# A graph network's second layer, written out: counts on four column groups, 15 block buffers in place of 6, two blocks used where they lie

## The reference

```python
h = maximum(layernorm(x), 0)
for W, b in ((W0, b0), (W1, b1)):              # the two layers
    h = hyp_linear(h, W, b)
    xt = logmap0(h)
    msg = xt[src] * w[:, None]
    agg = segment_sum(msg, dst)                # the sums over edges
    h = hyp_act(expmap0(agg))
x = x + h
h = maximum(layernorm(x), 0)
e = relu(concat([h[src], h[dst]]) @ W1 + b1) @ W2 + b2
counts = segment_sum(ones_like(dst), dst)      # edges of each destination
x = x + segment_sum(e, dst) / clip(counts, 1)
```

## Time and profile before

| | |
|---|---|
| time, median of 3 runs | 1238.22 us (1237.97 to 1239.96) |
| the profiled execution: its time, its span | 1235.21 us, 1233.2 us |
| TensorE busy | 1074.5 us (87%) |
| VectorE busy | 845.4 us (69%) |
| ScalarE busy | 598.8 us (49%) |
| second layer's groups, from first to last instruction | 529.5 to 651.7 us |
| mean traffic with HBM | 139 GB/s |

### The profile page before, as it was taken

How to read it: one execution, slowest core, us unless ns; L and a number is a source line. 1 busy time by engine, 2 the same in 40 slices (tenths; PEclk the granted TensorE clock), 3 DMA queues, 4 the chain that set the end, 5 groups by cost and what they waited for, 6 DMA issues and landing times.

```text
span 1233.2 us, 53744 instructions
## 1 busy us (share of the span) xinstructions
PE 1074.5 (87%) x22532; PEld 997.0 (81%) x22532; DVE 845.4 (69%) x1141; ACT 598.8 (49%) x1693; POOL 27.5 (2%) x28
## 2 busy tenths in 40 slices
PE   2089898988989888389997779999999999999998
PEld 2068777777777776279996579999999999999997
DVE  8889999999999995655555844444444444444442
ACT  5358888888888886300001643333333333333331
POOL 7000000000000000100000000000000000000000
PEclk9589999999999999689997779999999999999999
DMA  2003323223232233369970344444444444444440
GB/s 78 0 32 123 121 91 121 106 106 121 91 121 113 100 121 125 148 243 365 373 280 28 110 150 158 155 155 155 155 154 155 153 155 146 152 149 147 148 139 28
DMA packets 45160, 171.75 MB, mean 139 GB/s; under 512 B 19472, under 2 KB 19798, under 8 KB 45115
## 3 DMA queue, kind: packets, MB, share of 16 engines
q1 hardware_dynamic: 45115, 171.12, 38.7%
HBM read 122.95 MB, written 48.14 MB: 139 GB/s over the span
## 4 chain that ended last, share of the span: by engine, by line
PE 54%; DVE 30%; issue 8%; ACT 4%; DVEq 3%; DMA 0%; POOL 0%; ACTq 0%; POOLq 0%
PE PS L1419 17%; PE PS L1432 13%; PE PS L1421 11%; PE PS L1301 7%; DVE arena L963 6%; DVE arena L940 5%; DVE arena L948 4%; PE PS L1329 3%; DVE arena L926 3%; DVE arena L935 2%; DVEq L330 2%; ACT arena L594 1%; PE PS L1286 1%; PE PS L1377 1%; DVE Cw L755 1%
## 5 line engine op out<-in xcount | busy, mean ns | idle before, releaser
L1419 PE MATMUL PS<-arena 125*128 125x128 bf16 x3600 | 345.2, 219 | 6.8 <-ACT RT L699 6.3
L707 ACT ACTIVATE arena<-PS 128x512 f32<-128x512 f32 (+1 forms) x336 | 180.1, 551 | 319.5 <-PE PS L1421 319.5
L1164 DVE TENSOR_TENSOR arena<-ramp,slot_dst 128x1800 f32<-128x1800 f32 x48 | 97.6, 2033 | 251.2 <-PE PS L1432 250.7
L1419 PEld LDWEIGHTS PS<-arena 125*128 125x128 bf16 x3600 | 250.7, 97 | 10.8 <-issue 7.2
L1301 PE MATMUL PS<-arena,A 125*64 125x72 f32 x4800 | 177.8, 229 | 67.0 <-DVE aggTw L974 38.9
L1301 PEld LDWEIGHTS PS<-arena,A 125*64 125x64 f32 x4800 | 164.0, 138 | 76.5 <-DVE A L844 27.0
L594 ACT ACTIVATE arena<-arena 128x72 bf16<-128x72 bf16 x864 | 217.0, 344 | 1.9 <-DVE arena L948 1.9
L1421 PE MATMUL PS<-arena 108*128 108x128 bf16 x1200 | 167.4, 220 | 0.0
L1421 PE MATMUL PS<-arena,HTw 108*128 108x128 bf16 x1200 | 166.1, 219 | 0.0
L1432 PE MATMUL PS<-arena 128*64 128x72 f32 x4800 | 160.6, 227 | 0.4 <-DVE RT L1200 0.4
L1432 PEld LDWEIGHTS PS<-arena 128*64 128x64 f32 x4800 | 153.5, 137 | 5.5 <-DVE RT L1200 0.6
(11 more groups left out here) (182 smaller groups left out, 1048.1 us busy)
## 6 DMA issues: line engine op xcount, KB each, us to landing
adjacency<-arena SPq DMA_DIRECT2D x48, 900.0 KB, 3.6
arena<-adjacency SPq DMA_DIRECT2D x48, 900.0 KB, 5.2
Bw<-slot_rows SPq DMA_DIRECT2D x48, 800.0 KB, 4.2
Cw<-slot_rows SPq DMA_DIRECT2D x48, 700.0 KB, 4.9
arena<-q_table SPq DMA_DIRECT2D x144, 18.0 KB
q_table<-arena SPq DMA_DIRECT2D x6, 336.0 KB
slot_rows<-slot_row SPq DMA_DIRECT2D x49, 13.0 KB
x_sb<-in_x SPq DMA_DIRECT2D x1, 700.0 KB
```

The lines of the kernel that those rows point to most:

```text
L707: nc.scalar.activation(Hs[k][:, bs[0]:bs[-1] + 1, :], ts_ps[(k + q) % 2][:, 0:len(bs), :], ACT.Relu)\
L1164: nc.vector.tensor_tensor(Os[k], ramp[:, 1:1 + W].unsqueeze(1).broadcast_to([128, NB, W]), slot_dst[:, bass.ds(g, 1), :].rearrange("p g b ...
L1419: mm(ps, OTs[k][:, b, :], P3[:, b, part, :], start=(part == 0), stop=False)
```

## The change

The second layer is written out for all 48 groups on SP, TensorE and VectorE, and its order and buffers change:

- Groups 46 and 47 come first, and their blocks are read from `AB`, where the first layer left them (`KEPT`). The other 46 are loaded, in order, into 15 buffers in place of 6. These lie in the arena in front of and behind `AB`, over tables that only the first layer uses.
- The one-hots and their offsets (`OC`, `offb`) move from the arena into `Cw`.
- VectorE makes the one-hots of group i + 1 before it adds the sums and counts of group i.
- A count matmul has 32 columns of ones in place of one and writes to one of four 32-partition quarters of PSUM, in turn. There are two PSUM banks for the counts. `degree` becomes all 128 partitions of `RT`; its total is the sum of partitions 0, 32, 64 and 96, which the transposing matmuls of the end form with a vector `first_of`. There are 50 of these in place of 25.

```diff
-SECOND = 6
+SECOND = 15
-        degree = RT[0:1, :]
+        degree = RT[:, :]
+        kept = at[0] - 2 * NB * W
+        starts = list(range(0, kept - NB * W + 1, NB * W)) + list(range(at[0], ARENA - NB * W + 1, NB * W))
+        ABS = [arena[:, i:i + NB * W].rearrange("p (b w) -> p b w", w=W) for i in starts[0:SECOND]]
+        KEPT = [(g, AB[g % 2]) for g in (NG - 2, NG - 1)]
+        OC = [Cw[:, i * GT * HW:(i + 1) * GT * HW].bitcast(bf16).rearrange("p (t w) -> p t w", w=W) for i in range(2)]
-        cnt_ps = bank(3)[0:1, 0:W]
+        cnt_ps = [bank(2 + k)[:, 0:W] for k in range(2)]
...
+        def second_group(i):
+            return KEPT[i][0] if i < len(KEPT) else i - len(KEPT)
+        def second_buffer(i):
+            return divmod(i - len(KEPT), SECOND)
...
+            def load_blocks(i):
+                n, k = second_buffer(i)
+                if n:
+                    sp.wait_ge(applied2, nth(i - SECOND))
+                sp.dma_start(ABS[k].rearrange("p b w -> p (b w)"), a_d[second_group(i), :, :]).then_inc(a_in[k], 16)
...
+            ve.tensor_reduce(first_of[:, :], ident[:, 0:128:32], X, ALU.add)
...
-                def body(g, _, n, k):
-                    ve.wait_ge(cone_set, nth(g - 2))
+                def count_onehots(i):
+                    k = i % 2
+                    if i >= 2:
+                        ve.wait_ge(counted, nth(i - 2))
...
+                def add_group(i):
+                    base = window(ve, second_group(i))
+                    ve.wait_ge(applied2, nth(i))
+                    ve.wait_ge(added2, 2 * i + PRIMED)
...
+                count_onehots(0)
+                for i in range(NG):
+                    if i + 1 < NG:
+                        count_onehots(i + 1)
+                    add_group(i)
...
-                pe.wait_ge(added2, 2 * g + PRIMED)
+                if i >= 2:
+                    pe.wait_ge(added2, 2 * i - 2 + PRIMED)
                 for t in range(GT):
-                    last = mm(cnt_ps, onesb[:, 0:1], OC[k][:, t, :], start=(t == 0), stop=(t == GT - 1))
+                    quarter = slice(32 * (t % 4), 32 * (t % 4) + 32)
+                    last = mm(cnt_ps[k][quarter, :], onesb[:, 0:32], OC[k][:, t, :], start=(t < 4), stop=(t >= GT - 4))
...
             for b in range(NB):
-                last = mm(PS[0:PN, 3584 + b:3585 + b], degree[:, 0:N].rearrange("f (p b) -> f b p", b=NB)[:, b, :],
-                          ones[0:1, 0:1], start=True, stop=True)
+                for ps in node_halves:
+                    last = mm(PS[ps, 3584 + b:3585 + b], degree[:, 0:N].rearrange("f (p b) -> f b p", b=NB)[:, b, ps],
+                              first_of[:, :], start=True, stop=True)
```

More of the change, by code:

```diff
@@ L42 @@
 ATANH_MAXNORM = math.atanh(MAXNORM)
-ARENA = 30928
+ARENA = 30912
 ARTANH = [1.0 / k for k in (13, 11, 9, 7, 5, 3)]
@@ L119, in gnn_kernel @@
         y2s = sb("y2s", [128, 2])
+        first_of = sb("first_of", [128, 1])
         oki = sb("oki", [1, 2], i32)
@@ L148, in gnn_kernel @@
         AB = [carve(NB * W).rearrange("p (b w) -> p b w", w=W) for _ in range(2)]
[L150 to L153, removed]
+        kept = at[0] - 2 * NB * W
+        starts = list(range(0, kept - NB * W + 1, NB * W)) + list(range(at[0], ARENA - NB * W + 1, NB * W))
+        assert len(starts) >= SECOND
+        ABS = [arena[:, i:i + NB * W].rearrange("p (b w) -> p b w", w=W) for i in starts[0:SECOND]]
+        KEPT = [(g, AB[g % 2]) for g in (NG - 2, NG - 1)]
+        OC = [Cw[:, i * GT * HW:(i + 1) * GT * HW].bitcast(bf16).rearrange("p (t w) -> p t w", w=W) for i in range(2)]
+        offb = [Cw[:, 2 * GT * HW + i * GT:2 * GT * HW + (i + 1) * GT].bitcast(bf16).rearrange("p (t d) -> p t d", d=2)
+                for i in range(2)]
         fieldT = carve(TILES * FIELDS, bf16).rearrange("p (t f d) -> p t f d", f=FIELDS, d=2)
@@ L402, in _ @@
                     with sp.If(fast == 1):
-                        second_groups(sp, load_blocks)
+                        for i in range(len(KEPT), NG):
+                            load_blocks(i)
             def load_sources(g):
@@ L1016, in second_layer @@
             def second_layer():
-                def body(g, _, n, k):
-                    ve.wait_ge(cone_set, nth(g - 2))
-                    nc.vector.tensor_copy(offb[k], offT[:, bass.ds(g * GT, GT)].unsqueeze(2)
+                def count_onehots(i):
+                    k = i % 2
+                    if i >= 2:
+                        ve.wait_ge(counted, nth(i - 2))
+                    nc.vector.tensor_copy(offb[k], offT[:, second_group(i) * GT:second_group(i) * GT + GT].unsqueeze(2)
                                           .broadcast_to([128, GT, 2])).then_inc(cdloc_set, 1)
-                    ve.wait_ge(cdloc_set, nth(g))
-                    ve.wait_ge(counted, nth(g - 2))
+                    ve.wait_ge(cdloc_set, nth(i))
                     shape = [128, GT, HW, 2]
@@ L1029, in body @@
                                             ALU.is_equal).then_inc(cone_set, 1)
-                    base = window(ve, g)
-                    ve.wait_ge(applied2, nth(g))
-                    ve.wait_ge(added2, 2 * g + PRIMED)
+                def add_group(i):
+                    base = window(ve, second_group(i))
+                    ve.wait_ge(applied2, nth(i))
+                    ve.wait_ge(added2, 2 * i + PRIMED)
                     win = aggTw[:, bass.ds(base, W)]
-                    nc.vector.tensor_tensor(win, win, agg2_ps[k], ALU.add).then_inc(added2, 1)
-                    ve.wait_ge(counted, nth(g))
+                    nc.vector.tensor_tensor(win, win, agg2_ps[i % 2], ALU.add).then_inc(added2, 1)
+                    ve.wait_ge(counted, nth(i))
                     win = degree[:, bass.ds(base, W)]
-                    nc.vector.tensor_tensor(win, win, cnt_ps, ALU.add).then_inc(added2, 1)
-                second_groups(ve, body)
+                    nc.vector.tensor_tensor(win, win, cnt_ps[i % 2], ALU.add).then_inc(added2, 1)
+                count_onehots(0)
[3 more added lines that the diff above has]
+                    add_group(i)
                 ve.wait_ge(added2, 2 * NG + PRIMED)
@@ L1083, in any_order @@
                         if i < 2:
-                            win = degree[:, bass.ds(v * W, W)]
+                            win = degree[0:1, bass.ds(v * W, W)]
                             nc.vector.tensor_tensor(win, win, any_ps[F:F + 1, :], ALU.add)
@@ L1319, in first_body, with second_body @@
                 blocks(g, k)
[L1321 to L1326, removed]
-                pe.wait_ge(added2, 2 * g + PRIMED)
+            def second_body(i):
+                k = i % 2
+                if i >= len(KEPT):
+                    n, at_k = second_buffer(i)
+                    pe.wait_ge(a_in[at_k], 16 * (n + 1))
+                    adjacency = ABS[at_k]
+                else:
+                    adjacency = KEPT[i][1]
+                if i >= 2:
+                    pe.wait_ge(added2, 2 * i - 3 + PRIMED)
+                apply(applied2, agg2_ps[k], adjacency)
+                pe.wait_ge(cone_set, nth(i))
+                if i >= 2:
+                    pe.wait_ge(added2, 2 * i - 2 + PRIMED)
                 for t in range(GT):
-                    last = mm(cnt_ps, onesb[:, 0:1], OC[k][:, t, :], start=(t == 0), stop=(t == GT - 1))
+                    quarter = slice(32 * (t % 4), 32 * (t % 4) + 32)
+                    last = mm(cnt_ps[k][quarter, :], onesb[:, 0:32], OC[k][:, t, :], start=(t < 4), stop=(t >= GT - 4))
                 last.then_inc(counted, 1)
@@ L1363, in _ @@
                         pe.wait_ge(xt_set, 2)
-                        second_groups(pe, second_body)
+                        for i in range(NG):
+                            second_body(i)
                 with pe.If(fast == 0):
```

## The result

The changed kernel took 1240.8 us in the median of 20 runs (1238.9 to 1245.2), the kernel before 1239.2 in 20 runs beside it (1236.3 to 1241.0). The ratio is 1.002, with a 95% interval of 1.0012 to 1.0028: slower by 0.2%, where 22 us less had been forecast.

A forecast was written before the change was run, and what follows sets the result against it. TensorE, not the nearly saturated block loads, was taken to set the second layer's pace; 20.3 + 2.0 - 0.15 = 22.1 us off 1238.2 gave 1216.1 us, with an 8-in-10 range of 1212 to 1231.

The forecast's parts named there:

- Counts on four column groups: Second layer's 17 count matmuls per group overlap in four column groups, a group taking 2.04 us: 20.3 us saved.
- Rival 1: Count matmuls overlap, but starts stay 25 to 27 ns apart: 1229 to 1230.5 us; chance 0.25 including a milder form.
- The pauses between the halves and the counts: TensorE's pauses when switching between product and counts stay unchanged; bounds nothing and 0.1 us a group, taken as nothing.
- Everything written out: Second layer without its loop: entry and return costs go, 2.0 us gained, bounds 0 and 2.0.
- my own first term: The 20.3 us saving from count matmuls overlapping in four column groups, making the group 2.04 us.
- Rival 3: Code fetch becomes the bound in the written-out layer; 0.92 us lost per packet over 24 decides the sign; chance 0.05.
- One-hots ahead, second counting bank: VectorE prepares a group ahead and counts wait less: worth nothing at 2.45 us a group, necessary at 2.04.
- 15 buffers, two kept blocks: Block loads kept off the second layer's path with 13 us to spare; gives nothing alone, carries the counts' gain.
- Around it: Work outside the layer: one more small reduction before the layer norm loses 0.15 us; clearing and final transposes nothing.
- The clock: 1.2 GHz stretches ahead of the last loop may shift by 2 us, within the likeliest case's 1213 to 1221.

The follow-up runs named there:

- experiment 1: Changed kernel, but each reload into a used buffer moves 36 KB in place of 900, all instructions kept: 1218.3 us, ratio 0.984.
- experiment 5: Kernel before with only the counts on four column groups and the 128-partition degree (one PSUM bank, loop of six, 6 buffers): 1231.2 us, ratio 0.993.
- experiment 4: Changed kernel with 6 buffers and a loop again on TensorE and VectorE, 6 groups written out, then 7 passes of 6: 1225.8 us, ratio 0.989.
- experiment 3: Changed kernel, still written out, with 6 block buffers in place of 15: 1250.4 us, ratio 1.007.
- experiment 2: Changed kernel with its 17 count matmuls all in one 32-column group again, one behind the other: 1241.3 us, ratio 1.001.
- experiment 8: Changed kernel, written out with 15 buffers, but at most two reloads in flight: 1242.7 us, ratio 1.003.
- experiment 7: Changed kernel with a loop again, 8 groups written out, then 4 passes of 10, with 10 buffers: 1229.9 us, ratio 0.993.

## Why the prediction was wrong

- **Counts on four column groups, 20.3 us: right.** 17 counts take 0.34 us in place of 0.75, the product's starts are 2.04 us apart as forecast, and without heavy reloads the layer is 101.5 us (forecast 99). Rival 1, a floor of 25 ns between starts, did not come: 16 steps in 0.34 less the 0.2 of one matmul are 9 ns each. By the rule that the prediction cites from the Trainium skill ("TensorE: Matmul & The Clock Gate", section "Wait — 56ns, not 53.3ns?") the counts would have taken 0.43 us; starts in different column groups came closer together than it says. In the cold first group they took 0.48 in place of 1.18, as summed.
- **The pauses between the halves and the counts: right.** They stayed as they were, or 2.04 would not have come out.
- **"Everything written out", 2.0 us gained with a bound of 0: the step that failed.** It measured 19.5 us lost in stands, and even without heavy loads at most 0.6 of the 2.0 us came back (experiment 1). I read from the 12 written-out groups that packets cost nothing. But these 12 groups asked for only 6 packets, one in 4.9 us, and the price of code depends on the pace that my own first term had just changed: the 48 groups ask for 25 packets, at 2.04 us a group one in 3.9 us. No row of before shows packets coming at that rate beside loads, so the bound below had to be negative. Rival 3 named the mechanism and put its point of decision at 0.92 us a packet; the trace has 19.5 us of stands and slower products behind them, where 22.1 us turn the sign. Its chance of 0.05 was the error: it rested on a cover that the change itself took away.
- **One-hots ahead, second counting bank: harmless, but called necessary, and that was wrong.** VectorE waits 51 us for products in the layer and holds nobody up. But experiment 5 has neither and runs its later passes at the same 2.04 us a group, with the one-hots ready in time.
- **15 buffers, two kept blocks: no need.** No product waited for a block, but none does with 6 in experiment 4 either, nor in experiment 5, which also loads all 48 blocks, since the loads reach 420 GB/s. I had taken 2.25 us a block as the pace and held these buffers to be what carries the gain; what they do here is end the loads earlier, and in written-out code that is worth something: 1240.8 us against 1250.4 in experiment 3.
- **Around it: right.** The new reduction delays the layer norm by 0.07 us (7.67 for 7.60, forecast 0.15). The degrees' transposing matmuls run behind L1377 and nobody waits for them.
- **The clock.** A long stand can come before a fall of it: the product at 553.59 took 2.71 us with the clock at 0.61 in the window of 553.6 to 558, right behind a stand of 2.97 us. The stand of 2.73 us that is shown above had no such fall behind it. My range had the clock only behind the layer.

What stays open is why a packet starts later beside loads, even with two in flight, though its own transfer takes no longer: where the request waits is not shown. Nor was the least change run that these results point to, the counts alone with only six groups written out.

## What to carry to other kernels

Written-out code has a supply rate: here one 16 KB packet, about two groups, each 3.8 us when the DMA engines have little else to do (all that the code asked for, so the limit may lie higher), one in about 5 us beside a heavy stream. Before speeding up a dense stretch of matmuls, divide its new time by its packets and compare it with the rate the trace shows beside the same loads; a loop whose body is fetched once is the way out, and its returns (0.3 us) are cheap against a late packet (0.4 to 3 us). Give the loop as few written-out groups as it can have, but enough buffers that the loads can run ahead (six here, four were too few). An absence of idle time at the old pace is no proof for the new one.

## What the runs showed of the hardware

- Four column groups of 32 overlap fully for 72-column bf16 matmuls: a start each 9 ns, with weight loads of 32 columns in between.
- An instruction packet of 16 KB came each 3.8 us with thin loads (experiment 1) and each 4.9 to 5.25 us beside heavy ones: 16 in 84 us at 338 GB/s in the changed kernel, 17 at 344 in experiment 2, 17 at 296 in experiment 8. Its own transfer took 1.0 to 1.1 us in either case, and the stands of the changed kernel end 2.2 to 2.9 us after its start. The Trainium skill ("Runtime: NRT & Kernel Launch", section "Instruction fetch mechanics") has the fetch in 16 KB blocks, mostly hidden by the pace of dispatch. The trace agrees on the blocks; for TensorE beside loads it was not hidden: 14 stands of 0.4 to 3.0 us with 25 blocks.
- A loop body of ten groups, five packets of code at two groups each, ran its later passes without a packet (experiment 7, none from 586 to 645 us).
